# Adding the last two term slots of tiles 5 to 7 on POOL, in a convolution, gating and feed-forward kernel whose engine orders are written out anew

## The chip, the core and the metric

The kernel runs on one core of one Trainium2 chip. A core has five engines that each work through their own list in order: TensorE (PE, matrix products; its weight loads are shown apart as PEld), VectorE (DVE), ScalarE (ACT), GpSimd (POOL) and SyncE (SP, which here only issues DMAs). They meet through semaphores. The metric is the device time of one execution in microseconds (us); smaller is better.

## The reference: what is computed

The input `x` is 8 x 128 x 256, `ctx` has the same shape. With k = v = ctx and q = layernorm(x), each of the 16 heads (8 channels each) forms all products of two channels of k, convolves them causally over the 256 positions with the head's taps (an FFT in the reference), adds D times the product, multiplies by q and sums over one channel index:

```
kv  = einsum('bhil,bhjl->bijhl', k, v)
y   = causal_convolution(kv, ssm_kernel[h]) + kv * D[h]
out = einsum('bijhl,bhil->bjhl', y, q)
x   = x + out
gate = silu(layernorm(x) @ Wg.T); up = layernorm(x) @ Wu.T
x   = x + (gate * up) @ Wd.T        # Wg, Wu: 704 x 256, Wd: 256 x 704, int32 weights with scales
```

## The kernel before, in words

The 1024 rows of x are 8 tiles of 128 rows (`TILES`); a tile t holds two heads, 2t and 2t+1. Two tiles make a block of the feed-forward part (blocks i = 0 to 3), whose hidden dimension is cut into six chunks t = 0 to 5 (the last one half as high).

Each engine has one list of steps, written out by hand; what a step does is a helper, and the order of the calls is the order of the work. There is no planner in the program. A step waits only for the semaphores in its helper, but everything behind it on the same engine waits too.

**Convolution of head n.** POOL makes the products of channels (`pairs`, line 385), ACT the squares (line 480), DVE both for the first two heads (line 667). `direct(n)` (line 661, DVE) puts the D term into the Toeplitz matrix of heads 0 to 7. PE multiplies: `convolve_across` (line 983) and `convolve_within` (lines 992, 994), three products of two instructions each, into one of three PSUM buffers. For heads 8 to 15 the Toeplitz matrices come from a padded copy of the taps in HBM: POOL adds D to the taps (`add_skip_to_taps`, line 378), ACT stores them (line 547), and SP waits for that store before it issues the load of line 315, the weights and everything after.

**The query.** `stats_of_q`, `moments_of_q`, `variance_of_q` (DVE), `root_q` (POOL, line 369), `shift_of_q` (DVE, line 686), `norm_q` (ACT, line 486), `turn_q` (PE, line 937, a transpose), `evict_q` (ACT, lines 499 and 502).

**Terms.** `multiply_terms(n)` (DVE, lines 728, 731, 735) multiplies the convolution by q into `terms`, a buffer for each parity of the tile, with 8 slots of 128 columns in each of two halves. The sum over the 8 slots is the sum over a channel index. `wrap(t)` (ACT, line 511) copies columns that wrap around. Then:
- tiles 0 and 1: PE adds all 8 slots by turning (transposing) each into the same PSUM bank, in both halves: 16 instructions of line 963.
- tile 2: `merge_front` (line 281, slots in pairs, POOL) and `merge_back` (line 289) leave 4 slots, 8 turns.
- tiles 3 to 7: `merge_last` (DVE, line 298) leaves 2 slots, 4 turns. `merge_back` is on DVE up to tile 4 and on POOL from tile 5.

`sum_terms(t)` is the name of PE's step. `add_sum(t)` (DVE, line 692) adds its result to x.

**Feed-forward.** `stats_of_f` to `variance_of_f` (DVE), `root_f` (POOL, line 374), `shift_of_f` (DVE, line 709), `norm_f` (ACT, line 491), `turn_f` (PE, line 945), `high_f` (ACT, line 516) and `low_f` (DVE, line 714), which cut the turned rows into two 16-bit parts. `gates(i, t)` (PE, line 1016, 8 products, 4 for the last chunk), `gate` (ACT, line 520), `hidden_units` (DVE, line 743), `hidden_high` (ACT, line 525) and `low` (POOL, or DVE in a few chunks, line 259), `downs(i, t)` (PE, line 1035), `scale_out` (DVE, line 759), `add` (POOL, line 303), and the store.

Waits that the text below speaks of: `sum_terms(t)` waits for its merges, for `wrap(t)` and for a count that says that PSUM bank `turn` is free; `gates(i, t)` waits for `hidden_units` two chunks earlier, since the two chunks share a bank; `turn_f(t)` waits for `norm_f(t)` and for the `add_sum` or `low_f` that last read the bank `turn`; `multiply_terms(n)` waits for convolution n and for its q.

Of the kernel before, what the change touches and what calls it, by code (L numbers as in the profile page):

```python
# [9 lines left out]
ALU = mybir.AluOpType  # L10
ACT = mybir.ActivationFunctionType

P = 128
# [6 lines left out]
HALVES = L // P  # L20
# [25 lines left out]
TWICE_MERGED = 3  # L46
BACK_ON_POOL = [5, 6, 7]
# [27 lines left out]
def build(nc, x, ctx_skip, taps, wg_t, s_gate, wu_t, s_up, wd_t, s_down, taps_pad, out):  # L75
    with ExitStack() as ctx:
# [88 lines left out]
        all_merged = sem("all_merged")  # L165
        summed = sem("summed")
# [199 lines left out]
        def _(pool):  # L366
# [26 lines left out]
            def add(i, r):  # L393
# [16 lines left out]
            pairs(2, 1, 2)  # L410
            root_q(1)
            pairs(3, 0, 1)
            pairs(3, 1, 2)
            root_q(2)
            pool.wait_ge(k_loaded[3], 16)
            pairs(4, 0, 2)
            pairs(5, 0, 2)
            pairs(6, 0, 2)
            root_q(3)
            pairs(7, 0, 2)  # L420
            root_f(0)
            pool.wait_ge(k_loaded[4], 16)
            pairs(8, 0, 2)
            merge_front(nc.gpsimd, 2)
            root_q(4)
            pairs(9, 0, 2)
            root_f(1)
            pairs(10, 0, 2)
            root_q(5)
            pairs(11, 0, 2)  # L430
            pool.wait_ge(k_loaded[5], 16)
            pairs(12, 0, 2)
            root_q(6)
            merge_front(nc.gpsimd, 3)
            root_q(7)
            merge_front(nc.gpsimd, 4)
            low(0, 0)
            root_f(2)
            pairs(13, 0, 2)
            root_f(3)  # L440
            low(0, 1)
            low(0, 2)
            pairs(14, 0, 2)
            merge_front(nc.gpsimd, 5)
            pairs(15, 0, 2)
            merge_back(nc.gpsimd, 5)
            root_f(4)
            merge_front(nc.gpsimd, 6)
            low(0, 3)
            low(0, 4)  # L450
            merge_back(nc.gpsimd, 6)
            root_f(5)
            low(1, 0)
            low(1, 1)
            merge_front(nc.gpsimd, 7)
            low(1, 2)
            merge_back(nc.gpsimd, 7)
            root_f(6)
            add(0, 0)
# [5 lines left out]
            low(2, 2)  # L465
            add(0, 1)
            add(1, 0)
            add(1, 1)
            low(2, 3)
# [8 lines left out]
        def _(act):  # L478
# [75 lines left out]
            wrap(0)  # L554
            evict_q(1)
            act.wait_ge(k_loaded[3], 16)
            squares(4)
            norm_q(2)
            squares(5)
            squares(6)  # L560
            wrap(1)
            evict_q(2)
            squares(7)
            act.wait_ge(k_loaded[4], 16)
            squares(8)
            convert_gate()
            norm_q(3)
            wrap(2)
            squares(9)
            evict_q(3)  # L570
            norm_f(0)
            norm_q(4)
            convert_up()
            squares(10)
# [3 lines left out]
            squares(11)  # L578
            wrap(3)
            high_f(1)  # L580
            norm_q(5)
            convert_down()
            evict_q(5)
            act.wait_ge(scales_loaded, 3 * 16)
            gate(0, 0)
            wrap(4)
            gate(0, 1)
            hidden_high(0, 0)
            norm_q(6)
            hidden_high(0, 1)  # L590
            act.wait_ge(k_loaded[5], 16)
            squares(12)
            squares(13)
            gate(0, 2)
            evict_q(6)
            squares(14)
            hidden_high(0, 2)
            squares(15)
            gate(0, 3)
            norm_f(2)  # L600
            gate(0, 4)
            high_f(2)
            norm_f(3)
            high_f(3)
            hidden_high(0, 3)
            wrap(5)
            norm_q(7)
            gate(0, 5)
            gate(1, 0)
            evict_q(7)  # L610
            wrap(6)
            hidden_high(0, 4)
            norm_f(4)
            high_f(4)
            gate(1, 1)
            hidden_high(0, 5)
            hidden_high(1, 0)
            gate(1, 2)
            gate(1, 3)
            hidden_high(1, 1)  # L620
            wrap(7)
            norm_f(5)
            hidden_high(1, 2)
            gate(1, 4)
            high_f(5)
            gate(1, 5)
            hidden_high(1, 3)
            gate(2, 0)
            hidden_high(1, 4)
            hidden_high(1, 5)  # L630
            gate(2, 1)
            hidden_high(2, 0)
            hidden_high(2, 1)
            gate(2, 2)
            norm_f(6)
            hidden_high(2, 2)
            gate(2, 3)
            high_f(6)
            norm_f(7)
            gate(2, 4)  # L640
            hidden_high(2, 3)
            high_f(7)
            hidden_high(2, 4)
            gate(2, 5)
            hidden_high(2, 5)
            gate(3, 0)
            hidden_high(3, 0)
            gate(3, 1)
            gate(3, 2)
# [9 lines left out]
        def _(dve):  # L659
# [129 lines left out]
            moments_of_q(2)  # L789
            multiply_terms(1)  # L790
            variance_of_q(2)
            stats_of_q(3)
            dve.wait_ge(direct_loaded[3], 16)
            direct(4)
            direct(5)
            shift_of_q(2)
            moments_of_q(3)
            multiply_terms(2)
            variance_of_q(3)
            multiply_terms(3)  # L800
            add_sum(0)
            dve.wait_ge(x_loaded[3], 16)
            stats_of_q(4)
            stats_of_f(0)
            moments_of_q(4)
            dve.wait_ge(direct_loaded[4], 16)
            direct(6)
# [401 lines left out]
```

## Time and profile before

| | |
|---|---|
| median of 3 runs | 76.82 us (76.43 to 76.84) |
| the profiled execution | 76.37 us, of which the span of the profile is 74.6 us |
| PE busy | 68.8 us, 92% of the span, 469 matmuls |
| DVE, ACT, POOL busy | 62.0, 45.4, 58.6 us (83%, 61%, 79%) |
| DMA | 8.29 MB; 16 DMA engines 70% busy or more to about 24 us |
| chain that ended last | PE 60%, POOL 17%, DVE 11%, DMA 4%, issue 3%, ACT 2% |

A busy share is an average over the whole span, and stages differ. Idle time in front of an instruction is given in square brackets with what ended it. A matmul's end is modelled and overlaps the next by 0.16 us when PE works without a pause, so PE's speed is read from start to start. DVE's, ACT's and POOL's instructions overlap a little too; a distance from start to start is again what one costs.

### The profile page before, as it was taken

The page shows a single profiled execution, that of the slowest core. Times are in us where ns is not written, and L with a number is a line of the kernel's source. Part 1 is how long each engine was busy: PE and PEld are TensorE (multiplying, and loading weights), DVE is VectorE, ACT ScalarE, POOL GpSimd, SP SyncE. Part 2 cuts the span into 40 slices and gives each one's busy share as a digit, 9 for nine tenths or more (in the row PEclk, how much of TensorE's full clock was granted, in tenths as well). Part 3 has the DMA queues.
Part 4 walks back from the last instruction along what each step waited for, and adds up shares of the span by engine and source line. Part 5 has one row for each costly group of instructions (what it writes and reads, how often), then busy time and mean ns, then how long its engine had stood idle before and what let it go on. Part 6 is the DMA issues. An engine that isn't in the chain of part 4 may idle for free.

```text
span 74.6 us, 1493 instructions
## 1 busy us (share of the span) xinstructions
PE 68.8 (92%) x469; PEld 56.7 (76%) x469; DVE 62.0 (83%) x188; ACT 45.4 (61%) x115; POOL 58.6 (79%) x76
## 2 busy tenths in 40 slices
PE   4997979999999989999999999999999999999920
PEld 3754557988878848889798889797999989899810
DVE  0087899999988999999999899999968884686760
ACT  1503436460997879967746894647768796776300
POOL 6021787997999999899999999479998999339230
PEclk9999999999999999999999999999999999999999
DMA  1797998999999200000000000000002006000404
GB/s 8 194 194 225 400 291 267 370 388 399 367 355 303 78 7 0 0 0 4 9 0 0 0 0 4 0 0 0 0 13 70 0 0 211 0 9 0 141 0 141
DMA packets 7128, 8.29 MB, mean 111 GB/s; under 512 B 816, under 2 KB 6224, under 8 KB 7120
## 3 DMA queue, kind: packets, MB, share of 16 engines
q1 hardware_dynamic: 6912, 8.01, 33.8%
q10 hardware_dynamic: 208, 0.18, 0.8%
q8 instruction: 4, 0.07, 0.4%
q14 instruction: 4, 0.03, 0.1%
HBM read 7.12 MB, written 1.07 MB: 110 GB/s over the span
## 4 chain that ended last, share of the span: by engine, by line
PE 60%; POOL 17%; DVE 11%; DMA 4%; issue 3%; ACT 2%; POOLq 0%; DVEq 0%
PE conv L1016 26%; PE down L1035 13%; POOL products L385 10%; POOL rstd_q L369 4%; PE conv L983 4%; PE conv L994 4%; PE conv L992 4%; DMA x_sb<-x 4%; PE turn L963 3%; DVE terms L728 3%; PE turn L945 2%; PE turn L1035 2%; POOL terms L281 2%; DVE terms L731 1%; DVE stats_q L673 1%
## 5 line engine op out<-in xcount | busy, mean ns | idle before, releaser
L1016 PE MATMUL conv<-f_parts,wgu 128*128 128x256 f16 x176 | 22.1, 273 | 0.0
L385 POOL TENSOR_TENSOR products<-k_skip 128x512 f32<-128x512 f32 (+1 forms) x16 | 18.2, 1150 | 1.9 <-DMA k_skip<-ctx_skip 1.9
L1016 PEld LDWEIGHTS conv<-f_parts,wgu 128*128 128x128 f16 x176 | 16.6, 98 | 2.7 <-DVE hidden L743 0.3
L259 POOL TENSOR_TENSOR h_lo<-hidden,h_hi 128x256 fp32r<-128x256 f32 x18 | 13.1, 748 | 2.5 <-ACT h_hi L525 2.5
L743 DVE SCALAR_TENSOR_TENSOR hidden<-conv,su_sb,gate_act 128x256 f32<-128x256 f32 (+1 forms) x24 | 11.5, 482 | 3.0 <-ACT gate_act L520 2.7
L520 ACT ACTIVATE gate_act<-conv,sg_sb 128x256 f32<-128x256 f32 (+1 forms) x24 | 11.2, 468 | 4.1 <-PE conv L1016 3.9
L728 DVE TENSOR_TENSOR terms<-conv,q_ext 128x512 f32<-128x512 f32 x16 | 10.9, 681 | 0.4 <-PE conv L994 0.2
L992 PE MATMUL conv<-products,toeplitz 128*128 128x288 f32 x32 | 10.5, 411 | 0.5 <-DVE toeplitz L661 0.5
L983 PE MATMUL conv<-products,toeplitz 128*128 128x288 f32 x32 | 10.8, 420 | 0.1
L994 PE MATMUL conv<-products,toeplitz 128*128 128x288 f32 x32 | 10.4, 406 | 0.0
L525 ACT ACTIVATE h_hi<-hidden 128x256 fp32r<-128x256 f32 x20 | 8.3, 414 | 3.4 <-DVE hidden L743 3.1
L1035 PE MATMUL down<-wd,h_hi 128*128 128x256 f32 x35 | 9.7, 306 | 0.0
L731 DVE TENSOR_TENSOR terms<-conv,q_ext 128x384 f32<-128x384 f32 x16 | 8.8, 550 | 0.0
L1035 PE MATMUL down<-wd,h_lo 128*128 128x256 f32 x35 | 8.8, 279 | 0.0
L486 ACT ACTIVATE q_rows<-x_sb,shift_q,rstd_q 128x256 f32<-128x256 f32 x8 | 4.8, 596 | 6.2 <-DVE shift_q L686 6.2
L281 POOL TENSOR_TENSOR terms<-terms 128x512 f32<-128x512 f32 x6 | 8.4, 1398 | 0.0
L963 PE MATMUL turn<-ident,terms 128*128 128x128 f32 x60 | 7.9, 273 | 0.0
L992 PEld LDWEIGHTS conv<-products,toeplitz 128*128 128x128 f32 x32 | 5.8, 190 | 2.6 <-POOL products L385 0.9
L963 PEld LDWEIGHTS turn<-ident,terms 128*128 128x128 f32 x60 | 7.0, 141 | 0.9
L994 PEld LDWEIGHTS conv<-products,toeplitz 128*128 128x128 f32 x32 | 6.1, 190 | 1.7
L1035 PEld LDWEIGHTS down<-wd,h_hi 128*128 128x128 f32 x35 | 6.6, 189 | 0.5 <-DVE h_lo L259 0.2
L369 POOL TENSOR_TENSOR rstd_q<-variance_q,minus_half 128x1 f32<-128x1 f32 x8 | 5.3, 666 | 1.8 <-DVE variance_q L681 1.8
(65 smaller groups left out, 120.5 us busy)
## 6 DMA issues: line engine op xcount, KB each, us to landing
k_skip<-ctx_skip SPq DMA_DIRECT2D x3, 384.0 KB, 5.7
toeplitz<-taps_pad SPq DMA_DIRECT2D x2, 512.0 KB, 9.0
out<-x_sb SPq DMA_DIRECT2D x8, 128.0 KB, 1.7
toeplitz<-taps SPq DMA_DIRECT2D x3, 256.0 KB, 5.0
wg_int<-wg_t SPq DMA_DIRECT2D x1, 704.0 KB, 8.8
wu_int<-wu_t SPq DMA_DIRECT2D x1, 704.0 KB, 10.0
wd_int<-wd_t SPq DMA_DIRECT2D x1, 640.0 KB, 9.7
x_sb<-x SPq DMA_DIRECT2D x1, 512.0 KB, 6.6
```

Of the source, the lines that this page charges most:

```text
L259: eng.tensor_tensor(low_of(i, t), hidden[up_lanes(t), i % 2, t, :], high_of(i, t), ALU.subtract).then_inc(done, 1)
L281: eng.tensor_tensor(even, even, odd, ALU.add).then_inc(merged, 1)
L385: nc.gpsimd.tensor_tensor(view(products[:, n:n + 1], first * MADE + GROUP, [[MADE, halves], [GROUP, 4], [1, GROUP]]), view(k, 0, [[EXT * B ...
L520: nc.scalar.activation(gate_act[up_lanes(t), i % 2, t, :], gate_of(i, t), ACT.Silu, scale=sg_sb[gate_lanes(t), t:t + 1]).then_inc(gate_act ...
L728: dve.tensor_tensor(view(z, h, [[TERMS, HALVES], [P, 4], [to, GROUP]]), view(y, HALF0, [[COLS, HALVES], [GROUP, 4], [1, GROUP]]), view(q, ...
L743: dve.scalar_tensor_tensor(out=hidden[lanes, i % 2, t, :], in0=up_of(i, t), scalar=su_sb[lanes, t:t + 1], in1=gate_act[lanes, i % 2, t, :] ...
L963: done = nc.tensor.matmul(turned[:, c * P:(c + 1) * P], view(z, c * TERMS + slot, [[1, P]]), ident[:, :], is_transpose=True, start=(n == 0 ...
L983: nc.tensor.matmul(conv[BUFFER[n]][:, BANK:BANK + COLS], toeplitz[:, n, P:L], products[:, n, 0:COLS], start=True, stop=False)
L992: nc.tensor.matmul(y[:, BANK:BANK + COLS], within, products[:, n, MADE:MADE + COLS], start=False, stop=True)
L994: nc.tensor.matmul(y[:, HALF0:BANK], within, products[:, n, 0:COLS], start=True, stop=True).then_inc(conv_done, 1)
L1016: done = nc.tensor.matmul(bank_of(i, t)[:, n, :], wgu[:, c, column:column + P], f_parts[:, i % 2, part, c, :], start=(c == 0 and part == 0 ...
L1035: done = nc.tensor.matmul(down_of(i, r), part[:, r * P:(r + 1) * P], wd[:, t, :], start=own, stop=(t == FULL), skip_group_check=True)
```

## The change: what it does

A new step `merge_fully(t)` for t = 5, 6, 7 on POOL adds slot BACK to slot 0, in both halves (128 partitions x 256 numbers); `sum_terms` of those tiles waits for it and turns one slot in each half: 2 instructions of line 963 instead of 4. The orders of all four computing engines are written out anew, over their whole length; no other helper changes, and SP's list stays as it was.

```diff
+FULLY_MERGED = 5
+        def merge_fully(eng, t):
+            z = terms[:, t % 2, :]
+            first = view(z, 0, [[TERMS, HALVES], [1, P]])
+            wait(eng, all_merged, t + 1 - TWICE_MERGED)
+            eng.tensor_tensor(first, first, view(z, BACK, [[TERMS, HALVES], [1, P]]), ALU.add).then_inc(fully_merged, 1)
...
POOL, the start
+            pool.wait_ge(half_ready, 1)
+            root_q(0)
             pool.wait_ge(taps_loaded, 16)
             add_skip_to_taps()
-            pool.wait_ge(half_ready, 1)
-            root_q(0)
...
POOL, its new order from pairs(15)
             pairs(15, 0, 2)
             merge_front(nc.gpsimd, 5)
             merge_back(nc.gpsimd, 5)
             root_f(4)
             low(0, 2)
             merge_fully(nc.gpsimd, 5)
             low(0, 3)
             merge_front(nc.gpsimd, 6)
             merge_back(nc.gpsimd, 6)
             low(0, 4)
             root_f(5)
             low(1, 0)
             merge_fully(nc.gpsimd, 6)
             low(1, 1)
             low(1, 2)
             merge_front(nc.gpsimd, 7)
             merge_back(nc.gpsimd, 7)
             root_f(6)
             merge_fully(nc.gpsimd, 7)
             low(1, 3)
...
DVE, the start
+            dve.wait_ge(k_loaded[0], 16)
+            all_products(0, 0, 1)
             dve.wait_ge(x_loaded[0], 16)
             stats_of_q(0)
-            dve.wait_ge(k_loaded[0], 16)
-            all_products(0, 0, 1)
...
-            shift_of_q(0)
             dve.wait_ge(k_loaded[1], 16)
             all_products(1, 0, 1)
+            shift_of_q(0)
...
             variance_of_q(1)
+            dve.wait_ge(x_loaded[2], 16)
+            stats_of_q(2)
             dve.wait_ge(direct_loaded[2], 16)
             direct(2)
             direct(3)
-            dve.wait_ge(x_loaded[2], 16)
-            stats_of_q(2)
...
DVE, its new order from multiply_terms(14)
             multiply_terms(14)
             merge_last(dve, 6)
             shift_of_f(5)
             hidden_units(1, 2)
             low_f(4)
             multiply_terms(15)
             scale_out(0, 0)
             add_sum(6)
             hidden_units(1, 3)
...
PE, wait and turns of sum_terms
+                elif t < FULLY_MERGED:
+                    wait(pe, all_merged, t + 1 - TWICE_MERGED)
                 else:
-                    wait(pe, all_merged, t + 1 - TWICE_MERGED)
+                    wait(pe, fully_merged, t + 1 - FULLY_MERGED)
...
PE, its order around sum_terms(6)
             sum_terms(6, f_ready, 5)
             gates(1, 4)
+            turn_f(5, x1_ready, 7)
             gates(1, 5)
-            turn_f(5, x1_ready, 7)
             downs(1, 0)
             downs(1, 1)
-            downs(1, 2)
             gates(2, 0)
             gates(2, 1)
+            downs(1, 2)
             sum_terms(7, f_ready, 6)
```

Further moves that matter below: on PE `turn_q(5)` goes ahead of `turn_f(1)`, and `convolve(11)` behind `gates(0, 2)`; on POOL the `pairs` of heads 8 to 11 go ahead of the `root_f` and `merge_front` steps that stood between them; on DVE `merge_last(5)` goes ahead of `low_f(3)` and `multiply_terms(13)`; on ACT `squares(8)` goes behind `convert_gate`.

## Rows read from the trace of the kernel before

**Rows 1.** The page: busy time by engine, and TensorE's granted clock in 40 slices.
```profile
PE 68.8 (92%) x469; PEld 56.7 (76%) x469; DVE 62.0 (83%) x188; ACT 45.4 (61%) x115; POOL 58.6 (79%) x76
PEclk9999999999999999999999999999999999999999
```

**Rows 2.** Timeline to 10 us: start, duration, instruction, [idle before <- releaser].
```profile
1.05 3.42 PE L1055 MATMUL turn<-zeros 128*128 128x256 f16 x17 [1.05 <-DVE zeros L761]
...
4.31 0.18 POOL L378 TENSOR_TENSOR taps_sb<-taps_sb 16x1 f32<-16x1 f32 x1 [2.45 <-DMA taps_sb<-taps]
...
4.53 0.36 ACTq L547 DMA_DIRECT2D taps_pad<-taps_sb  x1
...
5.38 0.56 POOL L369 TENSOR_TENSOR rstd_q<-variance_q,minus_half 128x1 f32<-128x1 f32 x1 [0.88 <-DVE variance_q L681]
...
6.22 0.60 ACT L486 ACTIVATE q_rows<-x_sb,shift_q,rstd_q 128x256 f32<-128x256 f32 x1 [3.29 <-DVE shift_q L686]
...
9.40 0.61 DVE L661 SCALAR_TENSOR_TENSOR toeplitz<-anti,k_skip,toeplitz 128x128 f32<-128x128 f32 x2
...
9.89 0.72 PE L992 MATMUL conv<-products,toeplitz 128*128 128x288 f32 x2 [0.49 <-DVE toeplitz L661]
9.92 0.42 DVE L673 BATCH_NORM_STATS2 stats_q<-x_sb 128x6 f32<-128x256 f32 x1
```

**Rows 3.** Timeline, PE's one pause between 10 and 50 us.
```profile
27.18 0.41 PE L945 MATMUL turn<-ident,f_rows 128*128 128x128 f32 x2 [0.33 <-DVE f_parts L714]
```

**Rows 4.** Timeline, the turns of tiles 5 and 6 and PE's next step.
```profile
44.10 0.60 PE L963 MATMUL turn<-ident,terms 128*128 128x128 f32 x4
...
44.54 1.04 PE L1016 MATMUL conv<-f_parts,wgu 128*128 128x256 f16 x8
...
49.99 0.60 PE L963 MATMUL turn<-ident,terms 128*128 128x128 f32 x4
...
50.61 0.61 PE L1016 MATMUL conv<-f_parts,wgu 128*128 128x256 f16 x4
```

**Rows 5.** A group of instructions on POOL: busy us, mean ns | idle before.
```profile
L259 POOL TENSOR_TENSOR h_lo<-hidden,h_hi 128x256 fp32r<-128x256 f32 x18 | 13.1, 748 | 2.5 <-ACT h_hi L525 2.5
```

**Rows 6.** Line 289 on both engines: ns min/median/max, first and last start.
```profile
L289 DVE TENSOR_TENSOR terms<-terms x3: 661/681/693, 21.5 to 31.2; 128x512 f32<-128x512 f32 x3
L289 POOL TENSOR_TENSOR terms<-terms x3: 1281/1287/1288, 41.4 to 52.8; 128x512 f32<-128x512 f32 x3
```

**Rows 7.** Timeline, POOL beside a merge on DVE, twice.
```profile
21.49 0.66 DVE L289 TENSOR_TENSOR terms<-terms 128x512 f32<-128x512 f32 x1
21.52 1.04 POOL L369 TENSOR_TENSOR rstd_q<-variance_q,minus_half 128x1 f32<-128x1 f32 x1
...
43.03 0.68 DVE L298 TENSOR_TENSOR terms<-terms 128x512 f32<-128x512 f32 x1
...
43.19 1.66 POOL L281 TENSOR_TENSOR terms<-terms 128x512 f32<-128x512 f32 x1
```

**Rows 8.** Timeline, POOL and its waiters in the stage of tiles 5 to 7.
```profile
41.40 1.28 POOL L289 TENSOR_TENSOR terms<-terms 128x512 f32<-128x512 f32 x1
...
48.82 0.68 DVE L728 TENSOR_TENSOR terms<-conv,q_ext 128x512 f32<-128x512 f32 x1
...
48.98 0.55 POOL L374 TENSOR_TENSOR rstd_f<-variance_f,minus_half 128x1 f32<-128x1 f32 x1 [1.51 <-DVE variance_f L704]
...
54.22 0.69 DVE L298 TENSOR_TENSOR terms<-terms 128x512 f32<-128x512 f32 x1 [0.17 <-POOL terms L289]
...
55.42 0.60 PE L963 MATMUL turn<-ident,terms 128*128 128x128 f32 x4
```

**Rows 9.** Timeline, the load behind the stored taps and the first waiter for a weight.
```profile
9.46 0.47 SPq L315 DMA_DIRECT2D toeplitz<-taps_pad  x1
...
18.80 1.38 ACT L528 ACTIVATE wgu<-wg_int 128x1408 f16<-128x1408 int32 x1 [1.99 <-DMA wg_int<-wg_t]
```

**Rows 10.** DMAs issued between 8.9 and 9.0 us: KB, us to landing.
```profile
x_sb<-x SPq DMA_DIRECT2D x1, 512.0 KB, 6.6
```

More of the change, by code:

```diff
@@ L465, in _ @@
             low(2, 2)
+            add(0, 0)
+            low(2, 3)
             add(0, 1)
@@ L468, in _ @@
             add(1, 1)
-            low(2, 3)
             low(2, 4)
@@ L803, in _ @@
             stats_of_q(4)
+            stats_of_q(5)
+            moments_of_q(4)
             stats_of_f(0)
-            moments_of_q(4)
+            moments_of_q(5)
+            variance_of_q(4)
+            multiply_terms(4)
+            moments_of_f(0)
+            multiply_terms(5)
             dve.wait_ge(direct_loaded[4], 16)
             direct(6)
-            moments_of_f(0)
-            shift_of_q(3)
-            multiply_terms(4)
+            direct(7)
+            add_sum(1)
+            stats_of_q(6)
@@ L811, in _ @@
+            shift_of_q(4)
             variance_of_f(0)
-            direct(7)
-            variance_of_q(4)
-            multiply_terms(5)
-            add_sum(1)
-            shift_of_f(0)
-            stats_of_q(5)
-            stats_of_f(1)
-            stats_of_q(6)
-            moments_of_q(5)
-            moments_of_f(1)
-            merge_back(dve, 2)
-            shift_of_q(4)
-            moments_of_q(6)
-            variance_of_f(1)
+            variance_of_q(5)
+            stats_of_f(1)
@@ L826, in _ @@
+            stats_of_q(7)
+            moments_of_f(1)
+            moments_of_q(6)
+            merge_back(dve, 2)
+            moments_of_q(7)
+            variance_of_f(1)
+            shift_of_f(0)
+            variance_of_q(6)
+            shift_of_q(5)
             multiply_terms(6)
             add_sum(2)
-            stats_of_q(7)
+            multiply_terms(7)
+            variance_of_q(7)
+            shift_of_q(6)
+            low_f(0)
             shift_of_f(1)
-            moments_of_q(7)
@@ L847, in _ @@
+            add_sum(3)
+            merge_back(dve, 4)
+            moments_of_f(2)
+            stats_of_f(3)
+            variance_of_f(2)
+            moments_of_f(3)
             hidden_units(0, 1)
-            moments_of_f(2)
-            add_sum(3)
-            variance_of_f(2)
-            stats_of_f(3)
+            shift_of_q(7)
+            variance_of_f(3)
+            merge_last(dve, 4)
             multiply_terms(10)
-            moments_of_f(3)
+            hidden_units(0, 2)
+            add_sum(4)
@@ L854, in _ @@
             shift_of_f(2)
-            variance_of_f(3)
-            hidden_units(0, 2)
-            merge_last(dve, 4)
             multiply_terms(11)
-            add_sum(4)
             hidden_units(0, 3)
+            shift_of_f(3)
             stats_of_f(4)
-            shift_of_f(3)
+            multiply_terms(12)
+            moments_of_f(4)
+            low_f(2)
             hidden_units(0, 4)
-            low_f(2)
-            multiply_terms(12)
+            variance_of_f(4)
+            hidden_units(0, 5)
@@ L866, in _ @@
+            merge_last(dve, 5)
             low_f(3)
-            moments_of_f(4)
-            shift_of_q(7)
-            variance_of_f(4)
             multiply_terms(13)
-            merge_last(dve, 5)
+            low(0, 5)
+            add_sum(5)
+            hidden_units(1, 0)
+            stats_of_f(5)
             shift_of_f(4)
-            hidden_units(0, 5)
-            hidden_units(1, 0)
-            add_sum(5)
+            moments_of_f(5)
+            hidden_units(1, 1)
+            variance_of_f(5)
@@ L876, in _ @@
             multiply_terms(14)
[L877 to L879 removed]
+            merge_last(dve, 6)
+            shift_of_f(5)
+            hidden_units(1, 2)
             low_f(4)
[L881 to L883 removed]
             multiply_terms(15)
[L885 removed]
             scale_out(0, 0)
[L887 removed]
+            add_sum(6)
             hidden_units(1, 3)
[L889 removed]
```

215 lines of the change are left out of this document (101 added, 114 removed).

## The prediction, made blind

> **What bounds the kernel now.** I read the busy times and the clock first, then the chain of waits, then the timeline engine by engine. PE is busy 92% of the span at the full granted clock [rows 1]. The reader is to see that this is one engine kept full, not an average over full and empty stages: from 10 us to the end of the matmuls at 71.3 us I find only these pauses. One is 0.33 us before `turn_f(1)` at 27.18, by starts 0.49 us, released by `low_f(0)` on DVE [rows 3]. One follows `sum_terms(6)`: the four turns of tile 5 take 44.54 - 44.10 = 0.44 us from start to start, those of tile 6 take 50.61 - 49.99 = 0.62 us up to the next gates, so PE stood 0.18 us [rows 4]. A few tenths lie among the last products after 69.6. Before 10 us PE waits twice: for the first q, and until 9.89 for `direct(2)` and `direct(3)` of DVE [rows 2]. So work taken off PE after 10 us is worth its full time if nobody makes PE wait in its place; and a delay before 10 us stays, until a later pause swallows it. Between 40 and 57 us POOL is nearly as full as PE: it has one pause, 1.51 us before `root_f(5)`, and `merge_last(7)` on DVE waits 0.17 us for it [rows 8].
>
> **The turns.** Tiles 5, 6 and 7 lose two turns each. A turn costs 0.44 / 4 = 0.11 us [rows 4], so PE loses 6 x 0.11 = 0.66 us of work, and with PE full that is -0.66 us.
>
> **The adds.** The trace shows no such add, but `low` on POOL has its size (two operands from SBUF, 128 x 256): 0.748 us mean [rows 5]. Steps follow each other a little closer, so I take 0.70 us; bounds 0.65 and, with the disturbance below, 1.1. Three cost POOL 2.1 us, more than its one pause of 1.5 us. They are on the path only where `sum_terms` waits for them, or where a step behind them is late.
>
> **What DVE's merges do to POOL.** `root_q(4)`, one column, took 1.04 us beside a merge on DVE, against 0.56 us alone [rows 7, 2]; a `merge_front` took 1.66 us beside `merge_last(5)`, against about 1.28 us for a POOL merge alone [rows 7, 6]. So a merge on DVE that falls wholly on a step of POOL costs POOL about 0.48 us, half covered about 0.25 to 0.38. The Trainium skill says this too: its GPSIMD Engine Reference, Key points, has GpSimd share its SBUF interfaces with VectorE and contend with DVE instructions that have two SBUF inputs. By that page, this trace agrees, with 1.04 against 0.56 us. Its section Engine selection advises VectorE for adds, GpSimd being about twice as slow with two inputs; line 289 agrees with 1.287 against 0.681 us [rows 6]. Were that the whole story the adds would lose 0.3 us each against an add on DVE; but DVE is no emptier than POOL.
>
> **The start.** Three moves delay the first q and one delays PE directly.
> - `root_q(0)` goes ahead of `add_skip_to_taps` on POOL. The root ran from 5.38 to 5.94; now the tap addition (0.18 us [rows 2]) ends near 6.02. ACT waits for it to issue the store of the taps (0.36 us), and only behind it does `norm_q(0)`: at about 6.44 instead of 6.22, +0.22 us.
> - `shift_of_q(0)` now stands behind `all_products(1, 0, 1)`, which needs a DMA that lands near 5.7. It would end near 6.34, inside the same 0.22 us. Putting the first product ahead of `stats_of_q(0)` gains under 0.1 us on this path, counted above.
> - `multiply_terms(0)`, which waits for the first q, starts 0.22 us later, and `direct(2)` stands behind it, now with `stats_of_q(2)` in between: one more 0.34 us from start to start (bounds 0.33 and 0.42, its duration [rows 2]). `direct(2)` goes from 9.40 to 9.96, and PE's `convolve_within(2)` from 9.89 to 10.45: **+0.56 us**. If the x tile it reads lands late (issued just after 4 us, landing by about 9.2) it would be more, but DVE reaches it at 9.6.
> - The stored taps reach SP later. The store was issued at 4.53 and SP went on at 9.46 [rows 2, 9], 4.9 us; issued at 6.05 it lands near 11.0, and everything that SP issues behind it (Toeplitz matrices, both gate weights, k of heads 12 to 15, scales, Wd) is issued 1.5 us later. I cost this at nothing: a load issued at 8.94 lands 6.6 us later, at 15.5 [rows 10], so the DMA engines have work in hand until then and what queues behind lands as before. Without that cover the first to be late is `convert_gate`, which already waited for its weights until 18.80 [rows 9]; but `squares(8)` and `wrap(2)` behind it are wanted only after 22 us, so even 1.5 us would be mostly hidden.
>
> **10 to 44 us.** I followed the new lists with the durations of the old rows. PE runs from 10.45 without a pause up to `turn_q(5)`: POOL is well ahead with the products (heads 8 and 9 are done before 20 us), and `merge_back(2)` ends just as PE comes to it, at 23.0. At `turn_f(1)` the chain `multiply_terms(7)`, `low_f(0)`, `shift_of_f(1)`, `norm_f(1)` ends at 27.8 with PE there at 27.5: a pause of 0.30 us in place of the 0.49 us [rows 3]. The delay is then 0.56 - 0.19 = **+0.38 us** (rounded up over the starts), and nothing changes it until tile 5, though `convolve(12)` and `downs(0, 0)` come within 0.1 us of having to wait.
>
> **44 to 57 us.** POOL starts `merge_back(5)` near 40.35 instead of 41.40 [rows 8], but with `low(0, 2)` still to do. `merge_last(5)` then falls on `root_f(4)` (+0.48), and `merge_fully(5)` ends near 44.0, 0.15 us after PE wants it: +0.15 - 0.22. `sum_terms(6)` gets its add in time and the 0.18 us of pause behind it goes: -0.22 - 0.18. By here PE is 0.1 us ahead of before (gates(1, 4) at 50.5 against 50.61). What is late next stands on POOL: the adds fill the old pause, so `root_f(5)`, free at 48.98 before [rows 8], comes behind `low(0, 4)` at 47.8 and runs beside `merge_last(6)`; `shift_of_f(5)`, `hidden_units(1, 2)` and `low_f(4)` stand on DVE ahead of `multiply_terms(15)`, which moves from 48.82 [rows 8] to 49.55. `add_sum(6)` follows it and `turn_f(5)`, now ahead of `gates(1, 5)`, waits for `add_sum(6)`: PE pauses 0.25 us, and 0.15 us more for `hidden_units(1, 3)`. `merge_last(7)` and `root_f(6)` both start when `merge_back(7)` ends, the root is held, and `merge_fully(7)` ends near 55.7, just as PE reaches it. `sum_terms(7)` saves its 0.22 us, and PE arrives at the next gates within 0.1 us of before (55.42 + 0.44 = 55.86 [rows 8, 4]).
>
> **The end.** `turn_f(7)` may wait 0.1 us for its chain through `root_f(7)`; the rest keeps its order in all that PE needs, and the tail of 3.3 us behind the last matmul is the same.
>
> **Sum:** +0.38 (start) - 0.66 (turns) - 0.18 (old pause) + 0.15 (tile 5) + 0.25 + 0.15 (`turn_f(5)`, gates) + 0.1 (`turn_f(7)`) = +0.19 us; I round to **+0.15**, as such pauses overlap in part. The profiled execution would go from 76.37 us (span 74.6, 1.8 around it) to 76.5. The median shown is 76.82, 0.45 above that execution, so the median after is 76.97; I say 76.9.
>
> **Rivals.**
> 1. *PE gets its whole gain.* If POOL is a few tenths earlier than I reckon, the pauses of the sum's second half (0.15 + 0.25 + 0.15 + 0.1) are not there: 0.38 - 0.66 - 0.18 = -0.46 us, 76.4; if `turn_f(1)` also comes in time, the whole old pause of 0.49 us swallows the start's delay and it is -0.77 us, 76.05. For it: POOL had 1.5 us free there. Against it: 2.1 us of adds go into it.
> 2. *Slower: POOL becomes the bound of tiles 5 to 7.* The chain `merge_back`, `root_f` beside `merge_last`, `merge_fully`, `sum_terms`, `add_sum` decides as soon as POOL reaches `merge_back(6)` later than 45.9; from there each 0.1 us late is 0.1 us of the time. One more disturbance of 0.48 us, or adds of 1.1 instead of 0.70 us for tiles 6 and 7 (+0.8), put it at +0.6 to +0.95: 77.4 to 77.8. For it: the lengthened steps of rows 7. Against: PE had no long wait for POOL anywhere after 10 us.
> 3. *Slower: the clock.* PE's pause before `convolve_within(2)` grows by half a microsecond. The granted clock never fell in this trace [rows 1], with a shorter pause there; the fill products at the start came 3.42 / 17 = 0.20 us apart [rows 2], those of gates, as wide, 0.11 us. If the pause brought that pace back for as long as the fill took, about 1.7 us are lost: 78.6.
> 4. *The change does not do what it says.* The two turns go out of PE's list, so this can only mean that PE waits in their place, which is rival 2.
>
> **Numbers.** About 0.5% (0.38 us) is what a measurement of this kernel can tell from no change. My forecast has 0.40, within 0.5%; rival 1 has 0.28, faster; rival 2 has 0.28 and rival 3 0.04, slower. The range, 76.1 to 77.7, takes in nearly all of rival 1 and most of rival 2 and leaves out the clock. The forecast's own range is 76.5 to 77.2.
>
> **What would show it.** In the new profile: `convolve_within(2)` at 10.4 to 10.5; `norm_q(0)` at 6.4; SP's line 315 near 11.0 with line 528 no later than 19; `turn_f(1)` near 27.8; 54 turns of line 963 instead of 60; POOL's root beside `merge_last(5)` and `merge_last(6)` about 1 us long; `multiply_terms(15)` after 49.3; a pause of PE before `turn_f(5)`; `sum_terms(7)` at 55.5 to 55.8. I am wrong if PE shows no pause from 44 to 57 us (rival 1), or if its pauses there add to over 0.9 us (rival 2).

## The result, and the profile after

The changed kernel takes 78.29 us (median of 4 runs, 77.98 to 78.69); the kernel before took 76.82 us beside it, the median of its three fast runs (a fourth, in the slow state, took 77.78 us). The ratio is 1.0218, with a 95% interval of 1.0179 to 1.0258: slower, where I had forecast 76.9 us. The profiled execution took 77.98 us, span 76.2.

The page of the changed kernel first: busy time and instructions, the granted clock, and the chain of waits by engine.

```profile
PE 68.9 (90%) x463; PEld 55.9 (73%) x463; DVE 63.7 (84%) x188; ACT 45.8 (60%) x115; POOL 61.6 (81%) x79
...
PEclk9999999999999999999999999999999999999999
...
DVE 42%; PE 23%; POOL 14%; DMA 7%; ACT 5%; issue 4%; SPq 2%; DVEq 0%
```

Against [rows 1] six turns are gone (469 to 463 on PE) and three adds have come (76 to 79 on POOL), as the change says, and the clock never fell. POOL has 3.0 us more of busy time for adds of 0.72 us each, and DVE has 1.7 us more with the same 188 instructions: both got slower at old work. The chain that ended last went 60% through PE before; now 42% of it is DVE and 23% PE. PE is still busy 90% of the span, but over long stretches it follows the others.

The start, from the timeline (start, duration, engine, line; idle before and its releaser in brackets), answers to [rows 2, 9]. Line numbers are those of the changed kernel:

```profile
6.49 0.60 ACT L497 ACTIVATE q_rows<-x_sb,shift_q,rstd_q 128x256 f32<-128x256 f32 x1 [3.54 <-DVE shift_q L697]
...
10.54 0.37 SPq L323 DMA_DIRECT2D toeplitz<-taps_pad  x1
...
10.64 0.72 PE L1005 MATMUL conv<-products,toeplitz 128*128 128x288 f32 x2 [0.85 <-DVE toeplitz L672]
...
19.57 1.38 ACT L539 ACTIVATE wgu<-wg_int 128x1408 f16<-128x1408 int32 x1 [2.36 <-DMA wg_int<-wg_t]
```

`convolve_within(2)` starts at 10.64, 0.75 us later than before. Of this, 0.16 us is a lengthening that I did not expect: `direct(2)` on DVE took 0.50 us instead of 0.34, begun at 10.00 beside POOL's pairs, which ended at 10.35.

The stage of tiles 3 and 4, DVE's merges (lines 291 and 300) beside POOL:

```profile
28.31 0.92 DVE L291 TENSOR_TENSOR terms<-terms 128x512 f32<-128x512 f32 x1
...
28.64 1.73 POOL L393 TENSOR_TENSOR products<-k_skip 128x512 f32<-128x512 f32 x1
...
30.75 0.67 DVE L300 TENSOR_TENSOR terms<-terms 128x512 f32<-128x512 f32 x1
...
30.90 1.66 POOL L283 TENSOR_TENSOR terms<-terms 128x512 f32<-128x512 f32 x1 [0.53 <-DVE terms L746]
...
32.51 0.68 DVE L291 TENSOR_TENSOR terms<-terms 128x512 f32<-128x512 f32 x1
32.52 1.80 POOL L393 TENSOR_TENSOR products<-k_skip 128x512 f32<-128x512 f32 x1
...
34.27 0.68 DVE L300 TENSOR_TENSOR terms<-terms 128x512 f32<-128x512 f32 x1
34.28 1.08 POOL L382 TENSOR_TENSOR rstd_f<-variance_f,minus_half 128x1 f32<-128x1 f32 x1
...
36.02 1.29 POOL L393 TENSOR_TENSOR products<-k_skip 128x512 f32<-128x512 f32 x1
36.11 0.19 PEld L1048 LDWEIGHTS down<-wd,h_hi 128*128 128x128 f32 x1 [0.36 <-POOL h_lo L261]
```

Undisturbed, POOL's pairs take 1.29 us (36.02), a merge 1.28 [rows 6] and the root 0.56 [rows 2]. Here four steps in a row took 1.73, 1.66, 1.80 and 1.08 us: 1.85 us more, each begun while a DVE merge ran. DVE pays once as well: its merge at 28.31 began while POOL's `merge_front(3)` was at work (27.41 to 28.68) and took 0.92 us instead of 0.68. The last of the four steps makes `low(0, 0)` late, and PE's weight load for `downs(0, 0)` waits at 36.11.

Then tiles 5 to 7, which answer to [rows 4, 8], and one collision near the end:

```profile
42.32 0.69 DVE L300 TENSOR_TENSOR terms<-terms 128x512 f32<-128x512 f32 x1 [0.53 <-POOL terms L291]
...
43.56 0.72 POOL L306 TENSOR_TENSOR terms<-terms 128x256 f32<-128x256 f32 x1
43.61 0.41 PE L948 MATMUL turn<-ident,q_rows 128*128 128x128 f32 x2 [0.17 <-DVE f_parts L725]
...
44.75 0.41 PE L976 MATMUL turn<-ident,terms 128*128 128x128 f32 x2
...
44.93 1.26 POOL L283 TENSOR_TENSOR terms<-terms 128x512 f32<-128x512 f32 x1
...
45.08 1.40 DVE L261 TENSOR_TENSOR h_tail<-hidden,h_tail 64x256 fp32r<-64x256 f32 x1 [0.35 <-ACT h_tail L536]
...
46.51 0.42 DVE L703 TENSOR_TENSOR x_sb<-x_sb,turn 128x256 f32<-128x256 f32 x1
...
50.95 0.67 DVE L739 TENSOR_TENSOR terms<-conv,q_ext 128x512 f32<-128x512 f32 x1
...
52.54 0.40 DVE L703 TENSOR_TENSOR x_sb<-x_sb,turn 128x256 f32<-128x256 f32 x1
...
53.09 0.41 PE L956 MATMUL turn<-ident,f_rows 128*128 128x128 f32 x2 [0.57 <-DVE x_sb L703]
...
57.04 0.42 DVE L261 TENSOR_TENSOR h_tail<-hidden,h_tail 64x256 fp32r<-64x256 f32 x1
...
57.18 0.44 PE L976 MATMUL turn<-ident,terms 128*128 128x128 f32 x2
...
70.84 0.57 DVE L261 TENSOR_TENSOR h_lo<-hidden,h_hi 128x256 fp32r<-128x256 f32 x1
...
71.46 0.38 PE L1048 MATMUL down<-wd,h_hi 128*128 128x256 f32 x1 [0.17 <-DVE h_lo L261]
```

Look at line 261 on DVE: the same instruction takes 1.40 us at 45.08 and 0.42 us at 57.04. The first is `low(0, 5)`, begun 0.15 us after POOL's `merge_front(6)`; it ends at 46.48, 0.29 us after POOL's step. An instruction of 0.42 us has lost a microsecond inside itself, and no idle time is shown for it. `add_sum(5)` (46.51) and `multiply_terms(15)` (50.95, against 48.82 [rows 8]) stand behind it, then `add_sum(6)` (52.54), and PE waits 0.57 us before `turn_f(5)`. `sum_terms(7)` starts at 57.18 instead of 55.42 [rows 8]. The last matmul starts at 72.60 instead of 71.02, so no more is lost on balance behind tile 7. There are collisions there too: DVE's `low` steps at 66.31, 69.08 and 70.84 took 0.61, 0.76 and 0.57 us instead of 0.42 beside POOL, and PE stands 0.32 us, by starts, for the last of them at 71.46.

### The profile page after: what moved, and what is told of

Read it like the earlier page. It is cut to its first block, busy times and chain, and to the rows that moved or that the text cites. A ratio compares the mean times of both kernels' runs of the same rounds, so it can differ in the third digit from the quotient of the medians.

```text
span 76.2 us, 1484 instructions
## 1 busy us (share of the span) xinstructions
PE 68.9 (90%) x463; PEld 55.9 (73%) x463; DVE 63.7 (84%) x188; ACT 45.8 (60%) x115; POOL 61.6 (81%) x79
## 4 chain that ended last, share of the span: by engine, by line
DVE 42%; PE 23%; POOL 14%; DMA 7%; ACT 5%; issue 4%; SPq 2%; DVEq 0%
PE conv L1029 12%; DVE terms L739 8%; PE down L1048 8%; DMA toeplitz<-taps 7%; DVE terms L742 6%; POOL products L393 4%; POOL terms L283 4%; DVE stats_q L684 3%; DVE toeplitz L672 3%; DVE hidden L754 2%; DVE terms L746 2%; POOL rstd_f L382 2%; DVE terms L291 2%; DVE x_sb L703 2%; DVE h_tail L261 2%
## 5 line engine op out<-in xcount | busy, mean ns | idle before, releaser
L393 POOL TENSOR_TENSOR products<-k_skip 128x512 f32<-128x512 f32 (+1 forms) x16 | 19.0, 1201 | 2.2 <-DMA k_skip<-ctx_skip 2.2
L976 PE MATMUL turn<-ident,terms 128*128 128x128 f32 x54 | 7.3, 275 | 0.0
L976 PEld LDWEIGHTS turn<-ident,terms 128*128 128x128 f32 x54 | 6.0, 141 | 0.9 <-issue 0.2
```

What stands on the lines that cost most here:

```text
L393: nc.gpsimd.tensor_tensor(view(products[:, n:n + 1], first * MADE + GROUP, [[MADE, halves], [GROUP, 4], [1, GROUP]]), view(k, 0, [[EXT * B ...
L976: done = nc.tensor.matmul(turned[:, c * P:(c + 1) * P], view(z, c * TERMS + slot, [[1, P]]), ident[:, :], is_transpose=True, start=(n == 0 ...
```

## The experiments

Theory A: a DVE instruction with two operands from SBUF and a POOL instruction don't slow each other down, they exclude each other: who starts first holds the other off until it is done, and this works in both directions. Rivals: B, the adds make POOL the bound; C, the start's delay goes through to the end; D, PE's earlier steps make up for it, so the start doesn't count. Ratios stand against the kernel before on the same chip (76.5 to 76.6 us); times in us are a difference of ratios times 76.8, and a difference of two ratios is uncertain by some 0.3 us.

### The orders without the adds, and the adds without the orders

```
 a1 = changed kernel:  FULLY_MERGED = 8; no merge_fully(5), (6), (7); four turns a tile
 a2 = kernel before:   + merge_fully(5) behind root_f(4), (6) behind merge_back(6), (7) behind root_f(6)
```

> The new orders of all engines, without the three adds on POOL; tiles 5 to 7 are turned in four instructions each again. Theory A (the new orders cost the time: POOL and DVE get into each other's way and the start is later; the adds are a small part of it): PE has 0.66 us of turns more and POOL 2.1 us less; I expect the time within 0.5 us of the changed kernel, about +1.0 to +2.0 us against the kernel before, and low(0, 5) on DVE (line 259 or 261, h_tail) still over 1 us long at its first start. Theory B (the adds fill POOL, and that alone makes PE wait): the time falls back to that of before or below it, within 0.4 us of it, and the pauses of PE between 43 and 54 us are gone.

> The kernel before with nothing but the three adds: on POOL merge_fully(5) behind root_f(4), (6) behind merge_back(6), (7) behind root_f(6), two turns for tiles 5 to 7; all other orders as before. Theory A: each add waits for DVE's merge_last and costs POOL about 0.7 us behind it; sum_terms(5) starts near 44.5 instead of 44.1 and sum_terms(7) near 55.7 instead of 55.4, and downs(1, 3) waits up to 0.4 us for low(1, 3); the turns give 0.66 us back: 0 to +0.6 us against the kernel before. Theory B: +1.0 to +1.6 us, as the changed kernel.

a1: 77.95 us, 1.0193 (1.0153 to 1.0234). The new orders alone cost nearly all of it, and in them the adds cost about what they save. `low(0, 5)` still took 1.28 us, as theory A expected. a2: 78.34 us, 1.0238 (1.0203 to 1.0272), 1.8 us more than the kernel before and above both expectations: the adds in the old orders cost as much as the whole change. POOL's `merge_back(6)` is late, `merge_last(6)` with it, and DVE's list behind:

```profile
48.58 0.69 DVE L300 TENSOR_TENSOR terms<-terms 128x512 f32<-128x512 f32 x1 [0.61 <-POOL terms L291]
...
51.62 1.48 PE L1029 MATMUL conv<-f_parts,wgu 128*128 128x256 f16 x12 [0.80 <-DVE hidden L754]
...
57.04 0.44 PE L976 MATMUL turn<-ident,terms 128*128 128x128 f32 x2 [0.35 <-POOL terms L306]
```

No merge or `low` of DVE is held off in a2 before 59 us; there one `low` takes 0.92 us. So in the old orders rival B holds up to tile 7, and the new ones spare that and pay elsewhere.

### Is it low(0, 5)?

```
 a3:  - low(0, 5)    + DVE memset of h_tail, behind the same wait    (its values are left out)
 b1:  - low(0, 5)    + the same subtraction, second operand from PSUM (turned), behind sum_terms(5)
                       (so this part of the result differs)
 b3:  low(0, 5) directly behind merge_last(6);  POOL: merge_fully(6) ahead of low(1, 0)
```

> The changed kernel, but DVE's low(0, 5) is replaced by a memset of the same 64 x 256 values at the same place (the low part of the last hidden chunk of block 0 is left out of the result). Theory A1 (DVE's low(0, 5) stands still for 1.0 us because POOL's merge_front(6) holds something that both need; add_sum(5) and all of DVE behind it are late by that): the stretch of 1.40 us goes to under 0.4 us, multiply_terms(15) comes near 49.8 instead of 50.95, PE's pause before turn_f(5) shrinks from 0.74 us to under 0.2, and the time falls by 0.5 to 0.9 us. Rival A2 (turn_f(5) is late because of POOL's order and root_f(5), not because of this instruction): the time falls by under 0.3 us.

> The changed kernel; DVE's low(0, 5) stands at its place with the same size and output, but its second operand comes from PSUM (the bank turn) instead of SBUF, and it waits for the turns of tile 5 as well (the low part of the last hidden chunk of block 0 is then another number than it should be). Theory A1 (DVE and POOL exclude each other while both read SBUF through what they share, and DVE with one operand in PSUM doesn't need it): the instruction takes 0.40 to 0.50 us beside POOL's merge_front(6) instead of 1.40, and the time falls by 0.9 to 1.4 us, to within 0.8 us above the kernel before. Rival A3 (the memset of the run before was faster because it was a shorter instruction without reads, or the 64-lane form is slow by itself): the instruction stays over 1 us and the time falls by under 0.4 us.

> The changed kernel with DVE's low(0, 5) moved directly behind merge_last(6), where POOL waits for that merge, and POOL's merge_fully(6) ahead of low(1, 0) so that it does wait there. The instruction is whole. Theory A1: it takes 0.42 us there, add_sum(5) comes a microsecond earlier than in the changed kernel, and the time falls by 0.9 to 1.4 us. Rival A2 (the place of the collision only moves on to merge_fully(6) and low(1, 0)): under 0.5 us.

a3: 76.90 us, 1.0054 (1.0029 to 1.008). Taking out one instruction of 0.42 us, with a memset of 0.27 us in its place, was worth 1.3 us (1.0218 - 1.0054 = 0.0164, of 76.8; 0.9 to 1.6 by the intervals), more than the 0.5 to 0.9 that I had expected. The pause before `turn_f(5)` is gone. b1: 77.70 us, 1.0163 (1.013 to 1.0196); its rows on DVE and POOL:

```profile
44.76 1.26 POOL L283 TENSOR_TENSOR terms<-terms 128x512 f32<-128x512 f32 x1
45.10 0.42 DVE L886 TENSOR_TENSOR h_tail<-hidden,turn 64x256 fp32r<-64x256 f32 x1 [0.55 <-PE turn L979]
...
48.42 0.72 POOL L261 TENSOR_TENSOR h_lo<-hidden,h_hi 128x256 fp32r<-128x256 f32 x1
48.53 1.17 DVE L300 TENSOR_TENSOR terms<-terms 128x512 f32<-128x512 f32 x1
```

Same size, same place, same POOL step beside it, one operand from PSUM: 0.42 us instead of 1.40. That is the clearest evidence for the mechanism. The time fell by only 0.4 us, where 0.9 to 1.4 was expected, as `merge_last(6)` now fell on a `low` of POOL and took 1.17 us: the freed time moved the collision. b3, in which nothing is left out: 77.37 us, 1.0118 (1.0086 to 1.0151), 0.8 us less than the changed kernel, which lies between the two expectations; `low(0, 5)` takes 0.42 us, and POOL's add beside it 0.98 us instead of 0.72:

```profile
48.86 0.42 DVE L261 TENSOR_TENSOR h_tail<-hidden,h_tail 64x256 fp32r<-64x256 f32 x1
48.91 0.98 POOL L306 TENSOR_TENSOR terms<-terms 128x256 f32<-128x256 f32 x1 [0.44 <-DVE terms L300]
```

The Trainium skill has this as a rule, which I had not weighed in the prediction: SBUF — State Buffer, section Who interferes with whom, says that an instruction of DVE with two SBUF inputs and one of GpSimd that reads SBUF take a shared pair of ports as an exclusive lock, that the other fully blocks, and that issue order decides who does. By that the trace agrees, in both directions, but for POOL's one-column roots: `merge_last(5)`, begun 0.16 us into a root, took 0.69 us all the same, and there the measurement decides.

### The start

```
 a4:  root_q(0) behind the tap addition again, shift_of_q(0) and stats_of_q(2) back in their old places
 b2:  the whole start of the kernel before: DVE to add_sum(0), ACT to squares(7), POOL to pairs(5),
      PE to sum_terms(0)
 b4:  b2 and b3 together
```

> The changed kernel with the moves of the first 11 us undone: POOL adds the skip to the taps ahead of root_q(0), DVE has shift_of_q(0) ahead of all_products(1, 0, 1) and direct(2), direct(3) ahead of stats_of_q(2); the rest as changed. Theory C (a delay before 10 us stays to the end): convolve_within(2) starts 0.4 to 0.7 us earlier than 10.64, and the time falls by 0.4 to 0.7 us. Rival D (DVE and POOL are the bound from 15 to 53 us for their own reasons and swallow it): convolve_within(2) is earlier, the time falls by under 0.2 us.

> The changed kernel with the whole order of the kernel before on DVE up to add_sum(0), on ACT up to squares(7), on POOL up to pairs(5) and on PE up to sum_terms(0), and the changed order behind it. Theory C (the start's delay stays to the end): turn_f(1) near 27.4 instead of 27.8 and the time down by 0.3 to 0.6 us. Rival D (what stands between 28 and 53 us sets the time by itself): turn_f(1) earlier, the time down by under 0.2 us.

> Both edits together: the start of the kernel before, and low(0, 5) behind merge_last(6). If they add, 1.2 to 2.0 us below the changed kernel, which is the kernel before within 0.4 us or a little below it. If D holds, no better than the moved low(0, 5) alone.

a4: 77.98 us, 1.0204 (1.0159 to 1.0249). b2: 78.31 us, 1.0241 (1.0208 to 1.0275). b4: 77.76 us, 1.0185 (1.0138 to 1.0233), no better than b3. None falls as theory C expected. PE, DVE and POOL in b2:

```profile
10.10 0.72 PE L1005 MATMUL conv<-products,toeplitz 128*128 128x288 f32 x2 [0.24 <-DVE toeplitz L672]
...
19.47 1.28 POOL L393 TENSOR_TENSOR products<-k_skip 128x512 f32<-128x512 f32 x1
...
20.05 0.86 DVE L672 SCALAR_TENSOR_TENSOR toeplitz<-anti,k_skip,toeplitz 128x128 f32<-128x128 f32 x1
...
21.05 0.48 PE L1005 MATMUL conv<-products,toeplitz 128*128 128x288 f32 x1 [0.67 <-ACT products L491]
...
28.28 0.33 PE L956 MATMUL turn<-ident,f_rows 128*128 128x128 f32 x1
```

PE reaches `convolve_within(2)` 0.54 us earlier than in the changed kernel (10.64), and reaches `turn_f(1)` 0.46 us later (27.82). The gain is lost at one place, and not to slack. `direct(6)` on DVE reads both operands from SBUF and began at 20.05, inside POOL's pairs; it took 0.86 us instead of 0.34. DVE then runs 0.46 us behind the changed kernel (`add_sum(1)` 21.09 against 20.63), and the convolution that PE stands for at 21.05 starts 0.14 us after `direct(6)` ends. The profile names ACT there, whose step is `squares(8)`, for a later head; at the same place in b4 it names the `toeplitz` of DVE. b4 meets the same collision (0.94 us at 19.88), and a4 meets one with `direct(3)` (0.82 us at 9.98). So these runs have rival D's outcome, but they do not part C from D: each took the start's delay out and put a new collision in. That the start's delay counts for nothing is not shown.

### Moving the collisions about

```
 c1 = b3:  low_f(3) ahead of merge_last(5)
 c2 = b3:  without the three adds (low(0, 5) behind merge_last(6))
 c4 = c1:  gates(1, 5) ahead of turn_f(5), hidden_units(1, 3) ahead of add_sum(6)
```

> b3_tail_moved with DVE's low_f(3) ahead of merge_last(5) (the kernel before has it earlier too). In b3 DVE stood 0.53 us before merge_last(5), which waits for POOL's merge_back(5), and PE's turn_q(7) stood 0.34 us for the low_f(3) behind it. If that pause of PE is on the path: turn_q(7) starts without a pause near 43.1 instead of 43.45, evict_q(7), add_sum(5) and multiply_terms(15) follow earlier, and the time falls by 0.2 to 0.5 us. If POOL's chain to merge_last(6) sets the time there in any case: under 0.15 us.

> b3_tail_moved without the three adds (four turns for tiles 5 to 7 again). It asks what the adds are worth once the 1.0 us stall is gone. If PE sets the time, taking the adds away costs 0.66 us of turns less what POOL gives back: +0.2 to +0.6 us. If POOL and DVE set it, it is even or gains up to 0.4 us, as between the changed kernel and a1_no_adds, where it was even.

> c1_lowf3_first with the order of the kernel before around turn_f(5): PE has gates(1, 5) ahead of it, DVE has hidden_units(1, 3) ahead of add_sum(6). In b3 PE stood 0.44 us before turn_f(5) for add_sum(6), and that one follows multiply_terms(15). If this order is a cost: the pause before turn_f(5) goes or shrinks to 0.1 us and the time falls by 0.2 to 0.4 us against c1. If gates(1, 5) then waits for hidden_units(1, 3) instead, under 0.1 us.

c1: 77.68 us, 1.0137 (1.0111 to 1.0163), no gain over b3. PE's pause before `turn_q(7)`, which it was to remove, is gone, and `merge_last(5)`, at 42.64 instead of 42.16 in b3, met a `low`:

```profile
42.57 0.72 POOL L261 TENSOR_TENSOR h_lo<-hidden,h_hi 128x256 fp32r<-128x256 f32 x1
42.64 1.20 DVE L300 TENSOR_TENSOR terms<-terms 128x512 f32<-128x512 f32 x1
```

DVE's start 0.07 us behind POOL's cost DVE 0.5 us. In the changed kernel it was ahead of this `low`, and POOL paid: 0.91 us instead of 0.72. c2: 78.48 us, 1.026 (1.0232 to 1.0287). Without the adds POOL has run ahead, so its `low` at 48.57 catches `merge_last(6)` (48.63, 1.22 us), and one that ends at 57.85 catches `low(1, 5)` (57.29, 0.85 us). In these orders the adds are worth 1.1 us (1.026 - 1.0118 = 0.0142; 0.8 to 1.4 by the intervals), more than any expectation; the turns are 0.66 of it. c4: 77.90 us, 1.0166 (1.0136 to 1.0197), no gain over c1: as its rival said, PE now waits for `hidden_units(1, 3)` before `gates(1, 5)` (0.32 us at 52.52), and again 0.36 us before gates at 54.79.

### A part of it on the kernel before

```
 d1 = kernel before:  hidden_units(1, 2) ahead of multiply_terms(15)
 c3 = d1:             + merge_fully(7) on DVE behind merge_last(7), two turns for tile 7
```

> A try at a version that beats both, from the kernel before: hidden_units(1, 2) goes ahead of multiply_terms(15) on DVE, so that gates(1, 4) finds it ready behind sum_terms(6) (the pause of 0.18 us), and tile 7 alone gets the last add, on DVE directly behind merge_last(7), where DVE then stood 0.35 us for the next gate; its turns fall to two. POOL gets nothing. Worked out: -0.18 - 0.22 = -0.4 us against the kernel before, if multiply_terms(15), 0.39 us later, delays neither merge_front(7) nor merge_last(7) by more than 0.1 us; if it does, 0.

> The kernel before, with one exchange alone: DVE does hidden_units(1, 2) ahead of multiply_terms(15). Theory A (DVE and POOL hold each other off; nothing else of the change matters): the 0.18 us pause of PE behind sum_terms(6) goes and no two-operand step of DVE falls on a longer one of POOL than before, so -0.2 us, ratio 0.994 to 0.999. Rival (TensorE already had what it needed and multiply_terms(15), 0.4 us later, makes turn_f(5) or a later step late): 0 to +0.4 us, ratio 1.000 to 1.005, as with the add of tile 7 on DVE, which came to 1.006.

c3: 76.90 us, 1.0059 (1.0037 to 1.008), slower than the kernel before, where I had expected a gain of 0.4 us or none. The gates of block 1 no longer wait, but the add met POOL's `add_ffn` and PE waited for it:

```profile
54.65 0.92 POOL L311 TENSOR_TENSOR x_sb<-x_sb,ffn_out 128x256 f32<-128x256 f32 x1
55.02 0.83 DVE L306 TENSOR_TENSOR terms<-terms 128x256 f32<-128x256 f32 x1
...
55.91 0.44 PE L974 MATMUL turn<-ident,terms 128*128 128x128 f32 x2 [0.24 <-DVE terms L306]
```

d1: 76.46 us, 0.9998 (0.997 to 1.0027). The 0.18 us pause behind `sum_terms(6)` goes, but the 0.2 us that theory A expected is not seen. No version here beats the kernel before.

### What is left: tiles 3 and 4

```
 d2 = a3:  DVE's merge_back and merge_last of tiles 3 and 4 -> x * 1, same output, one SBUF operand
           (the sums of these tiles are left out)
 d3 = d2:  each twice, on the two halves that the merge would have read
```

> The changed kernel with the last low part of block 0 filled with zeros (as in the earlier experiment, which came to 1.0054), and with DVE's four merges of tiles 3 and 4 replaced by one multiplication by 1 each, of the same output, with one operand from SBUF (so the sums of tiles 3 and 4 are left out). Theory A: POOL's pairs at 28.6 and 32.5 us take 1.29 us instead of 1.74 and 1.80, merge_front(4) 1.28 instead of 1.66, the root 0.56 instead of 1.08; the pause before downs(0, 0) goes, and most of what is left over the kernel before: ratio 0.996 to 1.001. Rival (what is left comes from the orders of the start and of tiles 5 to 7, not from 28 to 36 us): 1.004 to 1.006. Neither says what DVE's time of one such multiplication is; if it is well under 0.68 us, the gain can also be DVE's, and the next kernel tells that.

> As the kernel with one multiplication in place of each of the four merges, but each done twice, on the two halves that the merge would have read, so that DVE is kept busy for longer while it still has one operand from SBUF. Theory A: POOL's steps are as short as there, and if the two take together about the 0.68 us of the merge, the ratio is within 0.002 of that kernel's. Rival (the gain there was DVE's own shorter time): the ratio is back at 1.004 to 1.006.

d2: 76.55 us, 1.0005 (0.9985 to 1.0025), 0.38 us less than a3 (0.1 to 0.6 by the intervals). The root at 34.31 takes 0.55 us and the pause before `downs(0, 0)` is gone, but two of POOL's steps were still long (1.46 us at 28.88, 1.39 us at 30.87), and DVE's multiplication at 32.58 took 1.20 us. d3: 79.32 us, 1.0334 (1.029 to 1.0379), far off both expectations:

```profile
28.34 0.65 DVE L293 TENSOR_SCALAR terms<-terms 128x512 f32<-128x512 f32 x1
28.68 1.45 POOL L403 TENSOR_TENSOR products<-k_skip 128x512 f32<-128x512 f32 x1
28.92 1.49 DVE L294 TENSOR_SCALAR terms<-terms 128x512 f32<-128x512 f32 x1
...
32.26 1.49 DVE L308 TENSOR_SCALAR terms<-terms 128x512 f32<-128x512 f32 x1
...
35.17 0.42 DVE L294 TENSOR_SCALAR terms<-terms 128x512 f32<-128x512 f32 x1
```

The multiplication was meant as a step that POOL cannot hold off, but POOL does. It takes 0.42 us for 512 columns when alone (a merge takes 0.68) and is held off like a merge: 1.49 us twice. So one operand from SBUF is not enough to be free of POOL. The Trainium skill says so, in the same section: `tensor_scalar` can enter a mode of DVE that uses both ports, and contends in it. By that the two times, 0.42 and 1.49 us, agree. d2 therefore gives a size for tiles 3 and 4, 0.4 us, but no upper bound, as it has collisions of its own; and it does not part POOL's delay from DVE's own shorter time.

## Why the prediction was wrong

- **"What DVE's merges do to POOL"** is the step that failed. It took POOL as the only one to be delayed, at about 0.48 us a merge. DVE is held off just as much when POOL starts first, and by the rest of POOL's step: 1.0 us for `low(0, 5)`. The sum had no term for it; a3 puts it at 1.3 us. I had seen no such row because the kernel before has none: each form of its two-operand steps from SBUF on DVE kept one length (merges 0.66 to 0.69 us, `low` 0.42, `direct` 0.32 to 0.35), since they happened to begin beside POOL's roots, in its pauses, ahead of its steps or within 0.12 us of their end. The trace showed one direction of an exclusion, and I took it for the whole.
- **"10 to 44 us"** said that nothing changes the delay. Two pauses came: 0.29 us before `downs(0, 0)` at 36.12, behind four lengthened steps of POOL, and 0.34 us before `turn_q(7)` at 43.61, behind `low_f(3)` (both by starts). The kernel before had lengthened steps there too, but with 0.70 us lost in all (at 29.02, 30.81 and 31.70 us: 1.52, 0.93 and 1.37, where 1.28, 0.56 and 1.28 are their own) against 1.85. I had placed these steps with their old durations.
- **"What bounds the kernel now."** That PE has almost no pause was true, and I took PE as the only bound. The slack of the chain through DVE and POOL behind it was tenths, not microseconds; I had noted `downs(0, 0)` within 0.1 us of waiting and gave it no price.
- **The start.** I forecast +0.56 us at `convolve_within(2)`, at 10.45; it came at 10.64, +0.75 us, of which 0.16 us is `direct(2)` held off. `norm_q(0)` came at 6.49 against 6.44, `turn_f(1)` at 27.82 against 27.8. The place was right and the size nearly. Whether the delay can be had back is open, as a4, b2 and b4 each lost it again to a new collision. SP's later loads cost nothing that I can see: `convert_gate` came 0.77 us later, at 19.57, and PE has no pause between 11 and 27 us.
- **The turns and the adds.** There are 54 turns, and the adds took 0.72 to 0.74 us (0.70 taken). In the changed kernel they cancel within the noise (a1 77.95 against 78.29 us).
- **"44 to 57 us."** `sum_terms(5)` came at 44.75 against about 44.0. `root_f(4)` took 0.57 us beside `merge_last(5)`, not 1 us, since it had started first, and `root_f(5)` was over before `merge_last(6)` began. `multiply_terms(15)` came at 50.95 against 49.55, and the pause before `turn_f(5)` came, 0.57 us (0.74 by starts) for 0.25. `sum_terms(7)` came at 57.18 against 55.5 to 55.8.
- **Rivals.** Rival 2 named the right side, but reached only 77.4 to 77.8 us, and had the wrong engine: not POOL's adds but DVE waiting for POOL. In the old orders its cause was right (a2), again at twice its size. Rival 3, the clock, did not happen.

An account that closes comes from where PE stood, read from start to start in the two profiled executions. Changed against before: +0.75 us before `convolve_within(2)`, -0.24 at `turn_f(1)` (0.25 instead of 0.49), +0.29 before `downs(0, 0)`, +0.34 before `turn_q(7)`, +0.19 before `turn_f(4)` at 48.46, -0.18 for the old pause, +0.74 before `turn_f(5)`, +0.32 at 71.46, and -0.66 for the turns. That is 1.55 us, and the last matmul starts 1.58 us later. In a3 the pauses of 0.19 and 0.74 us are gone and the others stay; its last matmul starts at 71.68, 0.92 us earlier than in the changed kernel. Against the prediction's sum: 0.51 for the start where it has 0.38, 0.34 for tile 5 where it has 0.15, 0.93 for `turn_f(4)` and `turn_f(5)` where it has 0.25 + 0.15, and 0.29 + 0.32 for which it has no term. The largest excess is the one that a3 traces to `low(0, 5)`. What each of the others would give back if it alone were removed stays open, and so does whether an order exists in which the adds pay.

## What to carry to other kernels

Where DVE and POOL both work on SBUF, lay the order so that a long POOL step and a two-operand DVE step never overlap, or give DVE's operand a place in PSUM: list each pair with its start times, since a few hundredths of a us decide which engine waits, and the wait can be as long as the rest of the other's step. In a profile, look for the same line with two durations; such a wait stands inside the instruction and shows no idle time. When you take one such collision out, look where the next one falls: in b1, c1, a4 and b2 the time gained was lost again in that way. Before a change that moves such steps, price each overlap in both directions, and don't take a full TensorE for the bound until the slack of what feeds it is known.

## What the runs showed of the hardware that I had not expected

- DVE, held off, ends its own time less 0.13 us after POOL's step: 46.48 after 46.19 for a step of 0.42 us, in c1 43.84 after 43.29 for one of 0.68. An overlap of 0.15 us cost nothing: `merge_last(6)` of the changed kernel began at 49.48, POOL's `low` ended at 49.63, and it still took 0.69 us.
- POOL's one-column roots hardly hold DVE off (`merge_last(5)` at 42.32, begun 0.16 us into a root of 0.57 us, took 0.69 us), while a DVE merge that starts first holds them off fully (1.08 us at 34.28).
- A subtraction of 64x256 took 0.42 us with one operand from PSUM and 1.40 us with both from SBUF, beside the same POOL step.
- A DVE multiplication with one SBUF operand, 0.42 us alone, took 1.49 us beside POOL.
- Three steps more on POOL made the kernel faster (c2 to b3, 1.1 us, of which 0.66 are turns). The rest goes with two collisions that c2 has (0.54 us at 48.63, 0.43 us at 57.29) and b3 has not; that they are the cause is argued, not shown.
